# Two-layer GroupNorm and 3x3 convolution on one core: how images travel between HBM and SBUF, and when the scaled weights are written

## The chip, the cores and the metric

One core of one Trainium2 chip. The metric is device time in microseconds (us) of one execution. The times shown are the median of three runs, and one more execution was taken with the profiler.

## The reference

64 images of 256 x 256 pixels with 16 channels, fp32, 4.19 MB an image. Two layers of the same kind follow each other:

```python
x = x + relu(conv3x3(gn(x), u0, v0, w0) + b0)   # gn: 8 groups, mean and variance over the whole image
x = x + relu(conv3x3(gn(x), u1, v1, w1) + b1)   # kernel ijkl = sum u[l,j] * w[l,k] * v[l,i]
```

Each layer needs the statistics of its whole input image before it can start. The kernel never normalises the pixels: it multiplies the weights by the inverse deviation and subtracts the mean's contribution as a bias.

## The kernel before

An image is held as 128 partitions, each with two image rows (`raw[128, a, 4096]`, where a, the row parity, is 0 or 1). DVE transposes 32x32 blocks of it into `N0` ("evens"), which layer 0 convolves; the sum of layer 0 goes to `T1` ("odds"), which layer 1 convolves; that layer's sum goes to `T2` ("result") and DVE transposes it back to `pixels`, whence it is stored.

Each layer of an image is cut into four **rounds** f = 0 to 3 (`conv0(p, f)`, `conv1(p, f)`), a round being 8 pairs of image columns in each of four quarters of the width. A round is: 96 products into `ps_y` on PE (L343 for layer 1, L301 for layer 0), the bias and ReLU on ACT from `ps_y` (L426, L423), 32 products on PE that bring the unconvolved pixels into `ps_x` (L368, L323), and on DVE the sum of both (`add`, L528 and L531). PE may write `ps_y` again once ACT has read it, and `ps_x` once DVE has read it. In the program each of these products is two matmul instructions with two weight loads, so PE executes about 512 instructions a round.

The order of one pass of the loop over p is written out by hand and is the same on all engines: four rounds of layer 0 on image p, during which DVE also turns image p + 1 in (`turn_in`, L515), and then four rounds of layer 1 on image p - 1, during which DVE turns the result out (`turn_out`, L543, two transposes a round, one for each parity).

In the rounds of layer 1 the statistics of the next images are worked in. At the middle of the 96 products (`HOOK_AFTER`) of round 1 PE does `group_sums(1, p)` and in round 2 `group_sums(0, p + 1)` (L256), and each waits there until DVE has reduced the partial sums (`reduce_partials`, L558 to L564), which it does behind `turn_out` of the round before. In rounds 1 and 2 DVE scales the weights (`scale_weights`, L580 to L588), also behind `turn_out`. With the scaled weights of layer 0 ACT writes the padding of the next image (`pad_evens`, L434) between its ReLU of round 2 and that of round 3.

The transfers are all issued by SP. `load(p)` waits until image p - 1 is wholly turned in and then issues 11 DMAs, ten of 12 partitions and one of 8, each partition's two rows (32 KB) in one contiguous piece. `store(p - 1)` waits until that image is wholly turned out and issues 11 of the same kind. `turn_in` waits for all of a load, and `turn_out` of round 0 for all of the store before. `GROUPS`, `STRIDE` and `ENGINES` (12) describe this split.

POOL adds chunks of the turned image for the mean (`folds`, L237, seven additions an image) and copies the halos.

Of the kernel before, what the change touches and what calls it, by code (L numbers as in the profile page):

```python
# [7 lines left out]
IMAGES, H, W, C = 64, 256, 256, 16  # L8
P = 128
Q = 32  # L10
QUADS = 4
# [6 lines left out]
EACH = 8  # L18
ROUNDS = SLOTS // EACH
HQ = H // QUADS  # L20
HALVES = 2
# [10 lines left out]
PRM = Q * (1 + SIDES + TAPS) + 1  # L32
CST = Q * (SIDES + SIDES + 1) + 2

ENGINES = 12
STRIDE = P // ENGINES
GROUPS = [slice(o, o + (ENGINES - 1) * STRIDE + 1, STRIDE) for o in range(STRIDE)] + [slice(ENGINES * STRIDE, P)]
IN_DMAS, OUT_DMAS = len(GROUPS), len(GROUPS)
TURNS = HALVES * ROUNDS + 1
HALO0, HALO1 = 2 * (QUADS - 1), QUADS  # L40
ODDS_SUM, ODDS_PAD = 1, 2
EVENS_SUM = 2
# [3 lines left out]
def freed(f):  # L46

    return slice(max(EACH * f - 1, 0), SLOTS if f == ROUNDS - 1 else EACH * (f + 1) - 1)
# [41 lines left out]
def build(nc, x, params, consts, out):  # L90
# [2 lines left out]
    ACT = mybir.ActivationFunctionType  # L93
    AX = mybir.AxisListType

    x_rows = x.rearrange("n (g a) w c -> n g (a w c)", a=HALVES)
    out_rows = out.rearrange("n (g a) w c -> n g (a w c)", a=HALVES)

    with ExitStack() as ctx:
        def sb(name, shape):  # L100
# [9 lines left out]
        pixels = sb("pixels", [P, HALVES, ROW])  # L110
# [29 lines left out]
        const_in = sem("const_in")  # L140
        zeros_set = sem("zeros_set")
        build_step = sem("build_step")
        image_in = sem("image_in")
        image_out = sem("image_out")
        turned_in = sem("turned_in")
        halo0 = sem("halo0")
        halo1 = sem("halo1")
# [21 lines left out]
        @block.sync  # L169
        def _(sp):  # L170
            for y in range(2):
                sp.dma_start(par[y][:], params[y]).then_inc(const_in, 16)
            sp.dma_start(cst[:], consts).then_inc(const_in, 16)

            def load(p):
                if p:
                    sp.wait_ge(turned_in, TURNS * p)
                for g in GROUPS:
                    sp.dma_start(raw[g, :, :].rearrange("p a x -> p (a x)"), x_rows[p][g, :]).then_inc(image_in, 16)

            def store(p):
                sp.wait_ge(turned_out, HALVES * ROUNDS * (p + 1))
                for g in GROUPS:
                    sp.dma_start(out_rows[p][g, :],  # L184
                                 pixels[g, :, :].rearrange("p a x -> p (a x)")).then_inc(image_out, 16)

            load(0)
            load(1)
            for p in range(IMAGES):
                if p + 2 < IMAGES:  # L190
                    load(p + 2)
                if p:
                    store(p - 1)
            store(IMAGES - 1)
            sp.wait_ge(image_out, 16 * OUT_DMAS * IMAGES)

        @block.gpsimd
        def _(pool):
# [280 lines left out]
        def _(dve):  # L479
# [26 lines left out]
                    make(nc.vector.tensor_tensor(pad, whole, pad, ALU.subtract))  # L506

            def turn_in(p, f):
                dve.wait_ge(image_in, 16 * IN_DMAS * (p + 1))
                if p:  # L510
                    dve.wait_ge(x_filled, round_of(0, p - 1, f) + 1)
                turned = N0[:, :, 1:1 + HQ].rearrange("p k (g a) -> p a k g", a=HALVES)
                for a in range(HALVES):
                    pixels_in = raw[:, a, :].rearrange("p (q k x) -> p q k x", q=QUADS, x=Q)
                    nc.vector.transpose(  # L515
                        turned[:, a, 1:1 + PAIRS, :].rearrange("p (q k) g -> p q k g", q=QUADS)[:, :, freed(f), :],
                        pixels_in[:, :, freed(f), :]).then_inc(turned_in, 1)
                if f == ROUNDS - 1:
                    nc.vector.transpose(turned[:, :, 0, :], raw[:, :, ROW - Q:ROW]).then_inc(turned_in, 1)

            def add(y, p, f):
                n = round_of(y, p, f)
                dve.wait_ge(relued, n + 1)
                dve.wait_ge(x_filled, n + 1)
                if y:
                    if ROUNDS * p + f:
                        dve.wait_ge(turned_out, HALVES * (ROUNDS * p + f))
                    nc.vector.tensor_tensor(T2[:].rearrange("p q k h -> p q (k h)"), ps_x[:], R[:],  # L528
                                            ALU.add).then_inc(added, 1)
# [73 lines left out]
            for p in range(IMAGES + 1):  # L603
                if p < IMAGES:
                    for f in range(ROUNDS):
                        if f == 0:
                            take_bias(0, p)
                        add(0, p, f)
                        if p + 1 < IMAGES:
                            turn_in(p + 1, f)  # L610
                for f in range(ROUNDS):
                    if p and f == 0:
                        take_bias(1, p - 1)
                    if p < IMAGES and f == ODDS_SUM:
# [8 lines left out]
                    if p < IMAGES and f == ODDS_SUM:  # L623
                        scale_weights(1, p)
                    if p + 1 < IMAGES and f == EVENS_SUM - 1:
                        reduce_partials(0, p + 1)
                    if p + 1 < IMAGES and f == EVENS_SUM:
                        scale_weights(0, p + 1)


def constants():
# [42 lines left out]
```

## Time and profile before

| | |
|---|---|
| median of 3 runs | 5731.84 us (5716.73 to 5732.2) |
| the profiled execution, its own time | 5744.38 us |
| its span | 5742.6 us |
| PE busy, matmuls | 4926.0 us, 86% of the span |
| DVE, ACT, POOL busy | 47%, 38%, 22% |
| the last chain, by engine | PE 73%, "issue" 15%, DVE 6%, ACT 3% |
| DMA queue q1 (images) | 537.22 MB, 37.7% of 16 engines |
| DMA queue q8 (instructions) | 17.94 MB in 1095 packets, 1.3% of 16 engines |

The time outside the span is 5744.38 - 5742.6 = 1.8 us. "issue" in the chain is time in which an engine waited for nothing that the profile names. The queue q8 is the one that brings the engines their instructions. A round can be followed by the start of its ReLU on ACT, of which there are eight an image.

### The profile page before, as it was taken

The numbers are of one execution on the slowest core, as the hardware profiler recorded it, in microseconds if no ns is written. First come the engines' busy times: TensorE is split into PE (matmuls) and PEld (weight loads), VectorE is DVE, ScalarE is ACT, GpSimd is POOL, SyncE is SP. The second block draws the span as 40 slices with busy tenths as digits, with TensorE's granted clock in tenths as the row PEclk, the third lists the DMA queues.
The fourth block names the chain that finished last, engine by engine and source line by source line (L and its number), as shares of the span: only waits on it lengthen the run. The fifth ranks groups of instructions, "written<-read, shape, count | busy, mean of one in ns | idle before, by whom it ended". The sixth has DMA issues, their size and how long they took to land.

```text
span 5742.6 us, 290853 instructions
## 1 busy us (share of the span) xinstructions
PE 4926.0 (86%) x139776; PEld 2691.7 (47%) x139776; DVE 2719.5 (47%) x3148; ACT 2197.5 (38%) x2242; POOL 1260.7 (22%) x1093
## 2 busy tenths in 40 slices
PE   4888988888888889889889888898888988888886
PEld 2444444444445444445445444454444544444543
DVE  3444444445444444445444444444444544455453
ACT  2443433434334344344344343343333433434332
POOL 2222212222122222122122221221212212222120
PEclk9999999999989999999999999999999999999998
DMA  4333443334333443343443343334433433344322
GB/s 91 91 91 91 105 107 91 91 91 116 96 91 92 107 103 94 95 109 96 102 109 91 95 112 96 91 94 109 99 91 91 113 99 91 91 100 111 91 69 84
DMA packets 34378, 555.84 MB, mean 97 GB/s; under 512 B 16432, under 2 KB 16816, under 8 KB 16816
## 3 DMA queue, kind: packets, MB, share of 16 engines
q1 hardware_dynamic: 33200, 537.22, 37.7%
q8 instruction: 1095, 17.94, 1.3%
q14 instruction: 83, 0.68, 0.0%
HBM read 268.72 MB, written 268.44 MB: 94 GB/s over the span
## 4 chain that ended last, share of the span: by engine, by line
PE 73%; issue 15%; DVE 6%; ACT 3%; SPq 0%; DMA 0%; DVEq 0%; ACTq 0%
PE ps_y L343 26%; PE ps_y L301 24%; PE ps_x L368 8%; PE ps_x L323 8%; PE ps_y L305 3%; DVE pixels L543 3%; DVE result L528 3%; ACT relu L426 2%; PE ps_y L275 2%; PE ps_x L256 1%; ACT evens L434 1%; DVE scaled L588 0%; ACT relu L423 0%; SPq L184 0%; PE ps_x L266 0%
## 5 line engine op out<-in xcount | busy, mean ns | idle before, releaser
L343 PE MATMUL ps_y<-odds,scaled 32*32 32x512 f32 x49152 | 2025.2, 660 | 222.8 <-issue 217.7
L301 PE MATMUL ps_y<-evens,scaled 32*32 32x512 f32 x46080 | 1801.1, 601 | 92.3 <-issue 79.9
L343 PEld LDWEIGHTS ps_y<-odds,scaled 32*32 32x32 f32 x49152 | 899.3, 108 | 1117.9 <-issue 739.3
L528 DVE TENSOR_TENSOR result<-ps_x,relu 128x2048 f32<-128x2048 f32 x256 | 586.6, 2291 | 1472.6 <-PE ps_x L368 1016.7
L426 ACT ACTIVATE relu<-ps_y,bias 128x2048 f32<-128x2048 f32 x256 | 503.7, 1967 | 1802.3 <-PE ps_y L343 1634.9
L531 DVE TENSOR_TENSOR odds<-ps_x,relu 128x2048 f32<-128x2048 f32 x256 | 586.7, 2292 | 1278.3 <-PE ps_x L323 952.9
L301 PEld LDWEIGHTS ps_y<-evens,scaled 32*32 32x32 f32 x46080 | 825.9, 103 | 699.6 <-issue 297.1
L237 POOL TENSOR_TENSOR fold<-fold,evens 128x1024 f32<-128x1024 f32 x384 | 843.9, 2198 | 644.0 <-DVE evens L515 607.0
L368 PE MATMUL ps_x<-odds,constants 32*32 32x512 f32 x16384 | 840.2, 642 | 88.3 <-issue 80.6
L423 ACT ACTIVATE relu<-ps_y,bias 128x2048 f32<-128x2048 f32 x256 | 503.6, 1967 | 1027.2 <-PE ps_y L301 542.0
L323 PE MATMUL ps_x<-evens,constants 32*32 32x512 f32 x16384 | 775.1, 604 | 21.7 <-issue 21.3
L224 POOL COPY odds<-odds 32x256 f32<-32x256 f32 x256 | 101.4, 396 | 2969.9 <-DVE odds L531 2958.0
L515 DVE STREAM_TRANSPOSE evens<-raw 128x1024 f32<-128x1024 f32 (+2 forms) x512 | 627.9, 1270 | 25.1 <-DMA raw<-in_x 25.1
L543 DVE STREAM_TRANSPOSE pixels<-result 128x1024 f32<-128x1024 f32 x512 | 610.8, 1234 | 27.1 <-DMA out<-pixels 18.4
L399 ACT ACTIVATE junk<-odds 128x2048 f32<-128x2048 f32 x256 | 490.5, 1916 | 327.0 <-DVE odds L531 327.0
L368 PEld LDWEIGHTS ps_x<-odds,constants 32*32 32x32 f32 x16384 | 415.2, 106 | 305.9 <-issue 170.2
L399 ACT ACTIVATE junk<-evens 128x2048 f32<-128x2048 f32 (+2 forms) x256 | 487.7, 1905 | 0.8 <-DVE evens L515 0.5
L323 PEld LDWEIGHTS ps_x<-evens,constants 32*32 32x32 f32 x16384 | 365.0, 103 | 204.7 <-issue 88.3
L305 PE MATMUL ps_y<-evens,scaled 32*32 32x448 f32 x3072 | 405.9, 549 | 29.7 <-ACT relu L426 21.6
L256 PE MATMUL ps_x<-sums,constants 32*32 32x2 f32 x4096 | 61.1, 182 | 331.6 <-issue 270.1
L237 POOL TENSOR_TENSOR fold<-evens 128x1024 f32<-128x1024 f32 x64 | 152.9, 2389 | 698.5 <-DVE evens L515 698.5
L256 PEld LDWEIGHTS ps_x<-sums,constants 32*32 32x32 f32 x4096 | 50.0, 113 | 438.4 <-issue 428.0
(46 smaller groups left out, 1523.0 us busy)
## 6 DMA issues: line engine op xcount, KB each, us to landing
raw<-in_x SPq DMA_DIRECT2D x640, 384.0 KB
out<-pixels SPq DMA_DIRECT2D x640, 384.0 KB
raw<-in_x SPq DMA_DIRECT2D x64, 256.0 KB
out<-pixels SPq DMA_DIRECT2D x64, 256.0 KB
parameters<-in_params SPq DMA_DIRECT2D x2, 96.5 KB, 2.1
constants<-in_consts SPq DMA_DIRECT2D x1, 81.0 KB, 2.2
```

The source lines that it names most:

```text
L237: nc.gpsimd.tensor_tensor(to, chunk(0) if d == 1 else to, chunk(d), ALU.add).then_inc(folded, 1)
L301: done = nc.tensor.matmul(ps_y[part, r, :], w0[rows, t * Q:(t + 1) * Q], N0[rows, k:k + EACH, i:i + HQ], start=(t == 0), stop=(t == NTAP - 1))
L305: nc.tensor.matmul(ps_y[part, r, HQ:WIDE], w0[rows, t * Q:(t + 1) * Q], N0[rows, k + 1:k + EACH, i:i + HQ], start=(t == 0), stop=False, sk ...
L323: done = nc.tensor.matmul(ps_x[Q * q:Q * (q + 1), r, :], perm[Q * r:Q * (r + 1), side, :], N0[Q * r:Q * (r + 1), k:k + EACH, 1:1 + HQ], st ...
L343: done = nc.tensor.matmul(ps_y[Q * r:Q * (r + 1), q, :], w1[p % 2][Q * q:Q * (q + 1), t * Q:(t + 1) * Q], t1[Q * q:Q * (q + 1), k:k + EACH ...
L368: done = nc.tensor.matmul(ps_x[Q * r:Q * (r + 1), q, :], perm[Q * q:Q * (q + 1), side, :], t1[Q * q:Q * (q + 1), k:k + EACH, 1 + HQ * r:1 ...
L399: nc.scalar.activation(into, source, ACT.Square, accum_out=to).then_inc(squared, 1)
L426: ins = nc.scalar.activation(R[:], ps_y[:], ACT.Relu, bias=bias[:, 1:2])
L515: nc.vector.transpose(turned[:, a, 1:1 + PAIRS, :].rearrange("p (q k) g -> p q k g", q=QUADS)[:, :, freed(f), :], pixels_in[:, :, freed(f) ...
L528: nc.vector.tensor_tensor(T2[:].rearrange("p q k h -> p q (k h)"), ps_x[:], R[:], ALU.add).then_inc(added, 1)
L531: nc.vector.tensor_tensor(T1[p % 2][:, EACH * f:EACH * (f + 1), 1:1 + H].rearrange("p k (r h) -> p r k h", h=HQ), ps_x[:].rearrange("p r ( ...
L543: nc.vector.transpose(to[:, :, EACH * f:EACH * (f + 1), :], result[:, a, :, :].rearrange("p (q k) g -> p q k g", q=QUADS)).then_inc(turned ...
```

## The change

The transfers are cut by round and parity: one load or store moves, for one parity a, the column pairs of one round for all 128 partitions (128 x 4 pieces of 256 elements, 224 in the first and 288 in the last load of an image), 16 transfers an image instead of 22. SP issues one load and one store a round: the load once PE has finished the round before (`x_filled`), the store once PE has finished the round's 96 products (`y_filled`). Each transfer also waits for its own data to be ready or free, and for the last transfer of the same kind and parity. There is a semaphore for each parity. DVE waits for the piece that it is about to read or overwrite, for every transpose. On DVE, `scale_weights` moves from behind `turn_out` to ahead of it.

```diff
-            def load(p):
-                if p:
-                    sp.wait_ge(turned_in, TURNS * p)
-                for g in GROUPS:
-                    sp.dma_start(raw[g, :, :].rearrange("p a x -> p (a x)"), x_rows[p][g, :]).then_inc(image_in, 16)
+            def load(p, f, a):
+                if p >= IMAGES:
+                    return
+                if p:
+                    sp.wait_ge(turned_in, TURNS * (p - 1) + (TURNS if f == ROUNDS - 1 else HALVES * (f + 1)))
+                if ROUNDS * p + f:
+                    sp.wait_ge(image_in[a], 16 * (ROUNDS * p + f))
+                part = slice(Q * freed(f).start, Q * freed(f).stop)
+                sp.dma_start(raw[:, a, :].rearrange("p (q y) -> p q y", q=QUADS)[:, :, part],
+                             x_rows[p, a][:, :, part]).then_inc(image_in[a], 16)
+            def store(p, f, a):
...
+                sp.wait_ge(turned_out, HALVES * (ROUNDS * p + f) + a + 1)
+                if ROUNDS * p + f:
+                    sp.wait_ge(image_out[a], 16 * (ROUNDS * p + f))
...
+            def pass_on(n, loaded, stored):
+                if n:
+                    sp.wait_ge(x_filled, n)
+                load(*loaded)
+                sp.wait_ge(y_filled, n + 1)
+                store(*stored)
...
+                if p < IMAGES:
+                    pass_on(round_of(0, p, 0), (p + 1, 3, 1), (p - 2, 1, 1))
+                    pass_on(round_of(0, p, 1), (p + 2, 0, 0), (p - 2, 2, 0))
...
+                    pass_on(round_of(1, p - 1, 3), (p + 2, 3, 0), (p - 1, 1, 0))
...
             def turn_in(p, f):
-                dve.wait_ge(image_in, 16 * IN_DMAS * (p + 1))
...
                 for a in range(HALVES):
+                    dve.wait_ge(image_in[a], 16 * (ROUNDS * p + f + 1))
...
             def turn_out(p, f):
-                if f == 0 and p:
-                    dve.wait_ge(image_out, 16 * OUT_DMAS * p)
                 for a in range(HALVES):
+                    if p:
+                        dve.wait_ge(image_out[a], 16 * (ROUNDS * (p - 1) + f + 1))
...
                     if p:
                         add(1, p - 1, f)
+                    if p < IMAGES and f == ODDS_SUM:
+                        scale_weights(1, p)
+                    if p + 1 < IMAGES and f == EVENS_SUM:
+                        scale_weights(0, p + 1)
+                    if p:
                         turn_out(p - 1, f)
```

What stands in SP's program for one image in the middle, before: a store and the next load, each of 11 DMAs in a row behind one wait.

```order
L184 DMA out<-pixels 12x8192 [waits turned_out]
L184 DMA out<-pixels 12x8192 x9
L184 DMA out<-pixels 8x8192
L179 DMA raw<-in_x 12x8192 [waits turned_in]
L179 DMA raw<-in_x 12x8192 x9
L179 DMA raw<-in_x 8x8192
```

And with the change, about four of the sixteen transfers of each pass:

```order
L179 DMA raw<-in_x 128x4x256 [waits image_in0,turned_in,x_filled]
L189 DMA out<-pixels 128x4x256 [waits image_out0,turned_out,y_filled]
L179 DMA raw<-in_x 128x4x256 [waits image_in1,turned_in,x_filled]
L189 DMA out<-pixels 128x4x256 [waits image_out1,turned_out,y_filled]
L179 DMA raw<-in_x 128x4x288 [waits image_in0,turned_in,x_filled]
```

Loads and stores now alternate, each behind a signal of PE. On DVE, rounds 2 and 3 of layer 1 before (the sum, the two transposes, then the four steps that scale layer 0's weights):

```order
L528 TENSOR_TENSOR result<-ps_x,relu 128x2048 [waits turned_out,x_filled,relued]
L543 STREAM_TRANSPOSE pixels<-result 128x4x256 [waits added]
L543 STREAM_TRANSPOSE pixels<-result 128x4x256
L580 TENSOR_SCALAR small<-small 128x1 [waits rooted]
L582 TENSOR_SCALAR small<-small 128x1 [waits norm_step]
L583 TENSOR_TENSOR scale<-small 128x1 [waits norm_step]
L588 TENSOR_SCALAR scaled<-weights,scale 128x448 [waits norm_step]
L528 TENSOR_TENSOR result<-ps_x,relu 128x2048 [waits turned_out,x_filled,relued]
```

The same place with the change (its line numbers are 36 higher):

```order
L564 TENSOR_TENSOR result<-ps_x,relu 128x2048 [waits turned_out,x_filled,relued]
L616 TENSOR_SCALAR small<-small 128x1 [waits rooted]
L618 TENSOR_SCALAR small<-small 128x1 [waits norm_step]
L619 TENSOR_TENSOR scale<-small 128x1 [waits norm_step]
L624 TENSOR_SCALAR scaled<-weights,scale 128x448 [waits norm_step]
L579 STREAM_TRANSPOSE pixels<-result 128x4x256 [waits image_out0,added]
L579 STREAM_TRANSPOSE pixels<-result 128x4x256 [waits image_out1]
L564 TENSOR_TENSOR result<-ps_x,relu 128x2048 [waits turned_out,x_filled,relued]
```

The four scaling steps have moved ahead of the two transposes, and each transpose has a wait of its own for a store.

## Rows read from the trace of the kernel before

**Rows 1.** The page: span, one DMA issue with KB each and us to landing.

```profile
span 5742.6 us, 290853 instructions
...
parameters<-in_params SPq DMA_DIRECT2D x2, 96.5 KB, 2.1
```

**Rows 2.** Stretches, load then store: PE, PEld, DVE, ACT, POOL busy; clock, DMA share, GB/s.

```profile
2296.00:2320.00 24.00, 15.80 (x430) 7.09 (x414) 11.20 (x18) 5.95 (x5) 7.19 (x9) 0.86 0.74 161
...
2343.00:2361.00 18.00, 15.35 (x455) 7.18 (x425) 8.99 (x6) 9.81 (x10) 2.00 (x5) 1.00 0.71 212
```

**Rows 3.** DMA queues, 2296 to 2320 us (a load): packets, MB, share.

```profile
q8 instruction: 3, 0.05, 1.0%
```

**Rows 4.** DMA queues, 2325 to 2341 us (no image moves).

```profile
q8 instruction: 4, 0.07, 1.7%
```

**Rows 5.** The chain, 2280 to 2400 us: start, us, what.

```profile
2301.26 1.99 issue
...
2304.77 3.09 issue
...
2357.08 1.85 issue
```

**Rows 6.** ACT in order of time, image from 5118.73 us: ReLU starts, padding.

```profile
5118.73 1.97 ACT L426 ACTIVATE relu<-ps_y,bias 128x2048 f32<-128x2048 f32 x1 [2.37 <-issue]
...
5145.60 1.97 ACT L426 ACTIVATE relu<-ps_y,bias 128x2048 f32<-128x2048 f32 x1 [13.45 <-PE ps_y L343]
...
5153.61 1.09 ACT L434 ACTIVATE evens<-zeros,moments 32x129 f32<-32x129 f32 x2 [4.61 <-DVE scaled L588]
5154.72 1.97 ACT L426 ACTIVATE relu<-ps_y,bias 128x2048 f32<-128x2048 f32 x1
...
5199.03 1.97 ACT L426 ACTIVATE relu<-ps_y,bias 128x2048 f32<-128x2048 f32 x1 [2.37 <-issue]
```

**Rows 7.** ACT: ReLU of layer 1, round 0, of the first and last image but one.

```profile
169.95 1.97 ACT L426 ACTIVATE relu<-ps_y,bias 128x2048 f32<-128x2048 f32 x1 [2.36 <-issue]
...
5634.51 1.97 ACT L426 ACTIVATE relu<-ps_y,bias 128x2048 f32<-128x2048 f32 x1 [2.37 <-issue]
```

**Rows 8.** The chain, 5118 to 5200 us.

```profile
5126.74 3.32 PE ps_y L343 x91
...
5135.55 3.73 issue
5139.28 0.37 PE ps_x L256 x22
5139.66 5.88 PE ps_y L343 x96
```

**Rows 9.** DVE in order of time, same image.

```profile
5139.04 0.15 DVE L559 TENSOR_REDUCE sums<-partial 128x1 f32<-128x4 f32 x1
...
5153.12 0.46 DVE L588 TENSOR_SCALAR scaled<-weights,scale 128x448 f32<-128x448 f32 x1
```

**Rows 10.** Busy time by stretch: round 1 to 2 of that image.

```profile
5130.10:5145.60 15.50, 11.77 (x306) 5.71 (x299) 7.44 (x14) 2.06 (x2) 0.00 (x0) 0.78 0.67 142
```

**Rows 11.** Busy time by stretch: round 0 to 1 of another image.

```profile
3874.40:3887.10 12.70, 10.72 (x305) 5.78 (x294) 5.77 (x10) 4.09 (x4) 7.37 (x9) 0.87 0.74 163
```

**Rows 12.** DVE in order of time, start and end of the program.

```profile
32.96 9.13 DVE L515 STREAM_TRANSPOSE evens<-raw 128x896 f32<-128x896 f32 x8 [25.08 <-DMA raw<-in_x]
...
53.72 1.22 DVE L558 TENSOR_REDUCE sums<-fold 128x1 f32<-128x1024 f32 x1 [11.50 <-POOL fold L237]
...
5694.58 2.37 DVE L543 STREAM_TRANSPOSE pixels<-result 128x1024 f32<-128x1024 f32 x2 [18.38 <-DMA out<-pixels]
```

**Rows 13.** ACT, last image: ReLU of layer 1, rounds 0 and 3.

```profile
5671.74 1.97 ACT L426 ACTIVATE relu<-ps_y,bias 128x2048 f32<-128x2048 f32 x1 [6.83 <-PE ps_y L343]
...
5711.02 1.97 ACT L426 ACTIVATE relu<-ps_y,bias 128x2048 f32<-128x2048 f32 x1 [9.23 <-PE ps_y L343]
```

**Rows 14.** SP's issues at the end of the program.

```profile
5717.96 17.76 SPq L184 DMA_DIRECT2D out<-pixels  x11
```

More of the change, by code:

```diff
@@ L33 @@
 CST = Q * (SIDES + SIDES + 1) + 2
[L35 to L38, printed above, removed]
 TURNS = HALVES * ROUNDS + 1
@@ L94, in build @@
     AX = mybir.AxisListType
-    x_rows = x.rearrange("n (g a) w c -> n g (a w c)", a=HALVES)
-    out_rows = out.rearrange("n (g a) w c -> n g (a w c)", a=HALVES)
+    x_rows = x.rearrange("n (g a) (q w) c -> n a g q (w c)", a=HALVES, q=QUADS)
+    out_rows = out.rearrange("n (g a) (q w) c -> n a g q (w c)", a=HALVES, q=QUADS)
     with ExitStack() as ctx:
@@ L142, in build @@
         build_step = sem("build_step")
-        image_in = sem("image_in")
-        image_out = sem("image_out")
+        image_in = [sem(f"image_in{a}") for a in range(HALVES)]
+        image_out = [sem(f"image_out{a}") for a in range(HALVES)]
         turned_in = sem("turned_in")
@@ L173, in _ @@
             sp.dma_start(cst[:], consts).then_inc(const_in, 16)
-            def load(p):
+            def load(p, f, a):
+                if p >= IMAGES:
+                    return
                 if p:
-                    sp.wait_ge(turned_in, TURNS * p)
-                for g in GROUPS:
-                    sp.dma_start(raw[g, :, :].rearrange("p a x -> p (a x)"), x_rows[p][g, :]).then_inc(image_in, 16)
[L181 to L191, printed above, removed]
-                if p:
-                    store(p - 1)
-            store(IMAGES - 1)
-            sp.wait_ge(image_out, 16 * OUT_DMAS * IMAGES)
+                    sp.wait_ge(turned_in, TURNS * (p - 1) + (TURNS if f == ROUNDS - 1 else HALVES * (f + 1)))
+                if ROUNDS * p + f:
+                    sp.wait_ge(image_in[a], 16 * (ROUNDS * p + f))
@@ new lines, in load @@
+                part = slice(Q * freed(f).start, Q * freed(f).stop)
+                sp.dma_start(raw[:, a, :].rearrange("p (q y) -> p q y", q=QUADS)[:, :, part],
+                             x_rows[p, a][:, :, part]).then_inc(image_in[a], 16)
+            def store(p, f, a):
+                if p < 0:
+                    return
+                sp.wait_ge(turned_out, HALVES * (ROUNDS * p + f) + a + 1)
+                if ROUNDS * p + f:
+                    sp.wait_ge(image_out[a], 16 * (ROUNDS * p + f))
+                part = slice(Q * EACH * f, Q * EACH * (f + 1))
+                sp.dma_start(out_rows[p, a][:, :, part],
+                             pixels[:, a, :].rearrange("p (q y) -> p q y", q=QUADS)[:, :, part]
+                             ).then_inc(image_out[a], 16)
@@ new lines, in pass_on @@
+            def pass_on(n, loaded, stored):
[4 more added lines that the diff above has]
+                store(*stored)
+            for p in range(2):
+                for f in range(ROUNDS):
+                    for a in range(HALVES):
+                        if p == 0 or f < ROUNDS - 1 or a == 0:
+                            load(p, f, a)
+            for p in range(IMAGES + 1):
+                if p < IMAGES:
+                    pass_on(round_of(0, p, 0), (p + 1, 3, 1), (p - 2, 1, 1))
+                    pass_on(round_of(0, p, 1), (p + 2, 0, 0), (p - 2, 2, 0))
+                    pass_on(round_of(0, p, 2), (p + 2, 0, 1), (p - 2, 2, 1))
+                    pass_on(round_of(0, p, 3), (p + 2, 1, 0), (p - 2, 3, 0))
+                else:
+                    store(p - 2, 1, 1)
+                    store(p - 2, 2, 0)
+                    store(p - 2, 2, 1)
+                    store(p - 2, 3, 0)
+                if p:
+                    pass_on(round_of(1, p - 1, 0), (p + 2, 1, 1), (p - 2, 3, 1))
+                    pass_on(round_of(1, p - 1, 1), (p + 2, 2, 0), (p - 1, 0, 0))
+                    pass_on(round_of(1, p - 1, 2), (p + 2, 2, 1), (p - 1, 0, 1))
+                    pass_on(round_of(1, p - 1, 3), (p + 2, 3, 0), (p - 1, 1, 0))
+                else:
+                    load(p + 2, 1, 1)
+                    load(p + 2, 2, 0)
+                    load(p + 2, 2, 1)
+                    load(p + 2, 3, 0)
@@ L197, in _ @@
+            store(IMAGES - 1, 1, 1)
+            for f in (2, 3):
+                for a in range(HALVES):
+                    store(IMAGES - 1, f, a)
+            for a in range(HALVES):
+                sp.wait_ge(image_out[a], 16 * ROUNDS * IMAGES)
         @block.gpsimd
@@ L622, in _ @@
                         reduce_partials(1, p)
-                    if p < IMAGES and f == ODDS_SUM:
-                        scale_weights(1, p)
                     if p + 1 < IMAGES and f == EVENS_SUM - 1:
                         reduce_partials(0, p + 1)
-                    if p + 1 < IMAGES and f == EVENS_SUM:
-                        scale_weights(0, p + 1)
 def constants():
```

## The prediction

> **What bounds the kernel now.** I read the page first: PE is busy for 86% of the span and fills 73% of the last chain, so the rounds of PE set the time, and what matters is what stands between its products. Then ACT in order of time. The ReLU of layer 1's round 0 starts at 169.95 us in the first pass that has both layers and at 5634.51 in the last; 62 images lie between [rows 7], so an image takes (5634.51 - 169.95) / 62 = 88.14 us on average. But one image in that run took only 5199.03 - 5118.73 = 80.30 us [rows 6]. Nothing in the program differs between the two. The question is where the 7.84 us go.
>
> The chain of the end shows two kinds of "issue". One stands directly ahead of the group sums (2301.26, 1.99 us [rows 5]; 5135.55, 3.73 us [rows 8]): PE waits there for DVE. DVE ends its reduction at 5139.04 + 0.15 = 5139.19, and the group sums start at 5139.28 [rows 8, 9]. The other stands in the middle of a round's products, where the program waits for nothing: 3.09 us at 2304.77 and 1.85 us at 2357.08 [rows 5]. The first of these lies in a load, the second in a store [rows 2]. I looked at the queues there. In 24 us of the load q8 delivered 3 packets of instructions, in 16 us without image traffic it delivered 4 [rows 3, 4]: one in 8.0 us against one in 4.0. The program has 290853 instructions in 1095 such packets, 266 in each, and PE wants some 512 a round, so about 1.9 packets a round, one every 4.6 us. So PE runs out of instructions while the images' 32 KB pieces fill the DMA engines. A round that begins with such a hole, or a hole beside it, also shows a lower clock: 0.86 in that load, 1.00 in the store [rows 2].
>
> **Edit 1, transfers by chunk and parity.** It removes 22 DMAs an image and adds 16. Bytes are unchanged: 2 x 4.19 = 8.39 MB an image. No piece is longer than 1.15 KB where it was 32 KB, and no more than one load and one store of 0.52 MB are issued a round. At the rates of before, 161 GB/s and 212 GB/s [rows 2], a load takes 3.3 us and a store 2.5 us, so 5.8 us of a round of about 8.9 has image traffic, as against 4.19 MB / 161 + 4.19 MB / 212 = 46 of 88 us today. The total of the traffic is the same; what changes is how long an instruction packet stands behind it. Today it comes 4 us late (8.0 - 4.0). If what it waits for is a fixed number of pieces, the wait falls with the piece by 32; if it is everything queued, it waits for one load at most, 3.3 us, or for both, 5.8. The first end costs nothing. At the other end the delay would be about that of today, but once in a transfer and not for a whole 24 us load, with a quiet stretch behind it in which the queue catches up. I take no loss, because the store, whose pieces leave faster, already starves PE less (15.35 of 18 us busy against 15.80 of 24 [rows 2]). So the stalls go: 7.84 us an image.
>
> The Trainium skill (Runtime: NRT & Kernel Launch, Instruction fetch mechanics) says that instructions come in 16 KiB blocks over the sequencer's own DMA queue and that the cost of a block is mostly hidden. The size agrees with this trace (0.07 MB in 4 packets [rows 4]), "mostly hidden" does not, by the 3.09 us. By that sentence the holes would have another cause and edit 1 would save only the ends of the program, as in the second rival below.
>
> What stays is worth as much care. In rounds 0 to 2 of layer 1 PE waits for DVE's partial sums even in the clean image: round 1 to 2 took 15.50 us [rows 10], of which 3.73 are that wait [rows 8]. DVE does the sum, `turn_out`, `scale_weights` and `reduce_partials` in a row; the change swaps the middle two, so the reduction ends at the same time and this wait stays. The 96 matmuls behind it took 5.88 us at the lower clock; the same piece of a round, after the shorter wait in round 0 to 1, took 3.32 [rows 8], and the stretch's mean clock was 0.78 [rows 10]. In another image round 0 to 1 fell too: 12.70 us at 0.87 [rows 11], where the clean image needed 26.87 - 15.50 = 11.37 [rows 6, 10]. These are PE's own idle times, not the DMA's, so I leave them in: the clean image is the forecast for every image. Its bounds are 80.30 - (5.88 - 3.32) = 77.74 if the clock holds, and 80.30 + 12.70 - 11.37 = 81.63 if it falls twice.
>
> New waits. Each load is issued seven rounds before `turn_in` needs it (three for the last piece of an image), each store at least three before `turn_out` needs its place: over 25 us for a transfer of about 3. SP's queue holds a store behind a load's waits; the longest of these is for `turn_in` in the round just begun, which DVE does within about 5 us, ahead of `y_filled`. Each second transpose now carries a wait that is long met; I count it as nothing to 0.1 us, twice an image on PE's path, at most 12 us in all.
>
> **Edit 2, weights scaled ahead of the transposes.** In round 2 DVE ends the scaling at 5153.12 + 0.46 = 5153.58 [rows 9], ACT pads from 5153.61 for 1.09 us, and the ReLU of round 3 starts at 5154.72, directly behind it [rows 6]. So padding holds up the ReLU. That round took 5154.72 - 5145.60 = 9.12 us, where the five behind it took (5199.03 - 5154.72) / 5 = 8.86 [rows 6], one of them with extra products. Two transposes earlier the padding falls where ACT is idle (4.61 us before it [rows 6]). Gain: 0.26 to, at most, the 1.09 of the padding; I take 0.35. The transposes move back by about 1.1 us, into the 5154.72 + 1.97 - 5153.58 = 3.1 us in which DVE now waits for the end of that ReLU [rows 6, 9]. In round 1 nothing waits for it.
>
> **The ends of the program.** At the start DVE waits for the whole first image until 32.96, and reduces at 53.72, 20.8 us later, held by POOL's additions [rows 12]. With chunks the additions can start after four of eight transfers, 2.1 MB, which at 161 GB/s is half of the time: about 13 us less, and the transposes run under the load, 5 to 9 us less. I take 20. At the end, `turn_out` of the last image waits 18.38 us for the store before [rows 12]; its last three rounds took 5711.02 - 5671.74 = 39.28 us [rows 13] where 3 x 8.86 = 26.6 would do: 12.7 less. The last store is issued from 5717.96 [rows 14] and the span ends 24.6 us later; two transfers of 0.52 MB need 5.0 us at 212 GB/s and 2.1 to land [rows 1], 7.0 in all: 17.6 less.
>
> **Sum**, against the profiled execution's own 5744.4 us: an image goes from 88.14 to 80.30 - 0.35 = 79.95, times 62 is 508; 508 + 20 + 12.7 + 17.6 = 558; 5744.4 - 558 = 5186 us. The profiled execution was 12.6 us above the median of the three runs (5731.84). I don't take this off: stalls that come and go are what the change should remove.
>
> **The rivals.**
> *Half of the stalls stay* (chance 0.14). Every instruction packet now meets traffic, where today half of them do. For: a round has 5.8 us of traffic, and two packets. Against: the store's shorter occupancy. Time: 5186 + 62 x 3.92 = 5429.
> *The holes are not the images' doing, or follow the bytes* (0.07). Then 7.84 us an image stays and only the ends and the padding are won: 5186 + 486 = 5672.
> *The clock holds* (0.07). With fewer holes PE arrives busier at the wait for the group sums: 5186 - 62 x 2.56 = 5027. Against: in the clean image it fell although nothing had starved PE just before.
> *Small pieces make the transfers the bound* (0.05), the slower side. The price of 1 KB pieces is in no row at this size. The nearest is 96.5 KB in pieces of 0.8 KB, landed in 2.1 us [rows 1], which is 46 GB/s if all of it grows with the bytes (11.4 us a transfer, two a round), and nearly free if it is a fixed delay. The other end is today's 161 to 212 GB/s. I take the latter, since that row moves a fifth of the bytes. The rival decides from 8.39 MB / 88.9 us = 94 GB/s, 5.6 us a transfer with none overlapped; at 90 GB/s an image takes 93.2 us: 5186 + 62 x 13.3 = 6008. The Trainium skill (DMA: Bandwidth & Descriptors, Rules for kernel authors) asks for 1 MiB or more in a DMA, which speaks against halves of that; by its fit of 2.0 us + bytes / 436 GB/s a transfer would be, as an estimate from that page, 3.2 us and sixteen 51 us, still under an image's 80.
>
> **How the numbers follow.** The forecast has 0.67, with a range of its own from 5100 to 5280 (the clock's 81.63 adds 104 at most if in every image, a clock that holds in half of the images takes 80). The range of eight in ten, 5080 to 5440, takes in the half-stalled case and leaves out the clock that always holds, the stalls that all stay and the slower case, 0.19 together. A difference under 0.3% (17 us) can't be told from none. Faster has 0.93, all but the slower case and a bit of the second rival; same 0.02; slower 0.05.
>
> **What would show it.** Right: ReLU starts of layer 1's round 0 about 80 us apart and evenly so; q8 with two packets a round throughout; no "issue" in the middle of a round's products; the wait ahead of the group sums still about 2 and 4 us; padding done before the ReLU of round 3 is due; group sums of the first image at about 34 us; 7 us from the last transpose to the end. Wrong: holes of a microsecond in the rounds that have a load, PE or DVE waiting for a DMA in the middle of the program, or SP issuing for more than a few us a transfer.

## The result: 5173 us against 5724

The changed kernel takes 5173.18 us (median of 4 runs, 5165.69 to 5176.38), the one before 5724.28 us beside it. The ratio is 0.9036, 95% interval 0.9015 to 0.9057. The profiled execution took 5165.69 us, with a span of 5163.9. (PE does the matrix products, DVE and POOL work element by element, ACT applies the ReLU, and SP issues the transfers.)

Lines of the page of the changed kernel: its engines, its last chain and two of its DMA issues (KB each, median us to landing):

```profile
span 5163.9 us, 291702 instructions
...
PE 4731.3 (92%) x139776; PEld 2677.6 (52%) x139776; DVE 2715.9 (53%) x3148; ACT 2198.9 (43%) x2242; POOL 1261.3 (24%) x1093
...
PE 88%; issue 9%; ACT 0%; DVE 0%; ACTq 0%; DVEq 0%
...
out<-pixels SPq DMA_DIRECT2D x512, 512.0 KB, 3.5
raw<-in_x SPq DMA_DIRECT2D x256, 512.0 KB, 3.9
```

"issue" went from 15% to 9% of the chain, and DVE (6%) and ACT (3%) have fallen under 1%. A transfer of 512 KB lands 3.5 to 3.9 us after its issue.

ACT in order of time: the ReLU of layer 1's round 0 in the first and the last of the 62 images, as in [rows 7]:

```profile
134.48 1.97 ACT L462 ACTIVATE relu<-ps_y,bias 128x2048 f32<-128x2048 f32 x1 [2.37 <-issue]
...
5088.39 1.97 ACT L462 ACTIVATE relu<-ps_y,bias 128x2048 f32<-128x2048 f32 x1 [2.37 <-issue]
```

An image takes (5088.39 - 134.48) / 62 = 79.90 us, 8.24 less, which is 511 of the 579 us between the two spans. The start gives 169.95 - 134.48 = 35.5, and what follows the last of these ReLUs 108.1 - 75.5 = 32.6. The images have also become even: each takes 78.3 to 82.3 us, where before they took 80.3 to 94.7.

The chain of one image of the changed kernel, from the sum of round 2 on:

```profile
2329.22 0.48 PE ps_y L341 x4
...
2334.55 0.51 issue
...
2339.86 5.99 PE ps_y L337 x168
...
2378.12 2.00 issue
2380.12 0.33 PE ps_x L292 x19
2380.45 4.71 PE ps_y L379 x88
...
2387.47 3.34 PE ps_y L379 x92
2390.81 3.60 issue
2394.41 0.33 PE ps_x L292 x18
2394.74 4.70 PE ps_y L379 x89
```

Read beside [rows 5, 8]: of the holes of up to 3 us in the middle of products one of half a microsecond is left in this image, in round 0 of layer 0 (2334.55). The two waits ahead of the group sums (L292) are what they were, 2.00 and 3.60 us, and the products behind them are slow in both rounds of this image (4.7 us; at the full clock 3.3). The stretches of the second wait and of the products behind it (us, then busy time of PE, PEld, DVE, ACT and POOL, granted clock, DMA share, GB/s):

```profile
2390.80:2394.40 3.60, 0.01 (x1) 0.03 (x1) 3.50 (x5) 0.00 (x0) 0.00 (x0) 1.00 0.00 0
2394.70:2399.60 4.90, 4.90 (x120) 3.11 (x125) 0.70 (x4) 0.00 (x0) 0.00 (x0) 0.65 0.01 3
```

PE is idle, DVE is not, no image moves, and after it the clock falls from 2.4 GHz to 1.2 for a part of the products (mean 0.65). Over the 62 images this fall follows the second wait in every one, and the first wait in 18 of them. Before, it came in 46 images in the round of the first wait and in 60 in that of the second (rounds with over 1 us at 1.2 GHz). The time at 1.2 GHz went from 9.9 us an image to 5.1.

The next table holds the mean time between two ReLUs, worked out from the ReLU starts on ACT of 62 images in each trace. Column "1-2" is from the ReLU of layer 1's round 1 to that of round 2, "3-0'" from layer 1's last to layer 0's first.

```
kernel                0-1    1-2    2-3    3-0'   0'-1'  1'-2'  2'-3'  3'-0   image
before              14.66  17.11   9.37   9.33   9.69   9.96   9.14   8.89   88.14
changed             11.68  14.47   8.75   9.77   8.79   8.76   8.76   8.92   79.90
scale only          14.68  17.07   8.91   9.34   9.65   9.94   9.03   8.89   87.50
transfers only      11.96  14.60   9.11  10.11   8.76   8.74   8.76   8.91   80.94
unpaced             12.17  15.57   9.15   9.44   8.77   9.49  10.12   8.98   83.67
burst, small        13.22  15.59   9.10   9.33  10.93   9.77   8.73   8.89   85.56
paced, long         13.60  15.23   9.20   9.81   9.71   9.02   9.23   9.35   85.15
pairs               12.15  14.33   8.95  10.52   8.93   8.79   8.94   9.05   81.67
quiet round         11.60  14.44   8.74   9.38   8.96   8.74   8.78   8.93   79.57
reduce first         9.45  10.63   8.80   9.83   8.74   8.76   8.80   8.98   73.98
reduce + quiet       9.50   9.84   8.87   9.48   9.00   8.78   8.79   8.97   73.24
later sums           9.17   9.31   9.19   9.42   9.04   8.77   8.79   8.97   72.67
```

### The profile page after: what moved, and what is told of

It is laid out like the page before. It is cut to its first block, busy times and chain, and to the rows that moved or that the text cites. A ratio compares the mean times of both kernels' runs of the same rounds, so it can differ in the third digit from the quotient of the medians.

```text
span 5163.9 us, 291702 instructions
## 1 busy us (share of the span) xinstructions
PE 4731.3 (92%) x139776; PEld 2677.6 (52%) x139776; DVE 2715.9 (53%) x3148; ACT 2198.9 (43%) x2242; POOL 1261.3 (24%) x1093
## 3 DMA queue, kind: packets, MB, share of 16 engines
q8 instruction: 1095, 17.94, 1.5%
## 4 chain that ended last, share of the span: by engine, by line
PE 88%; issue 9%; ACT 0%; DVE 0%; ACTq 0%; DVEq 0%
PE ps_y L379 35%; PE ps_y L337 26%; PE ps_x L404 11%; PE ps_x L359 9%; PE ps_y L341 4%; PE ps_y L311 2%; PE ps_x L292 1%; PE ps_x L302 0%; ACT relu L459 0%; PE ps_y L317 0%; ACT relu L462 0%; DVE result L564 0%; DVE pixels L579 0%; ACTq L457 0%; DVEq L95 0%
## 5 line engine op out<-in xcount | busy, mean ns | idle before, releaser
L379 PE MATMUL ps_y<-odds,scaled 32*32 32x512 f32 x49152 | 1876.0, 645 | 3.8 <-issue 0.5
L337 PE MATMUL ps_y<-evens,scaled 32*32 32x512 f32 x46080 | 1741.9, 598 | 11.6 <-issue 2.4
L379 PEld LDWEIGHTS ps_y<-odds,scaled 32*32 32x32 f32 x49152 | 879.0, 106 | 820.2 <-issue 414.8
L404 PE MATMUL ps_x<-odds,constants 32*32 32x512 f32 x16384 | 776.7, 606 | 0.0
L404 PEld LDWEIGHTS ps_x<-odds,constants 32*32 32x32 f32 x16384 | 425.8, 103 | 158.2 <-issue 23.2
L359 PEld LDWEIGHTS ps_x<-evens,constants 32*32 32x32 f32 x16384 | 383.8, 103 | 155.1 <-issue 28.0
L292 PE MATMUL ps_x<-sums,constants 32*32 32x2 f32 x4096 | 47.1, 182 | 391.7 <-issue 355.5
L292 PEld LDWEIGHTS ps_x<-sums,constants 32*32 32x32 f32 x4096 | 39.0, 112 | 503.2 <-issue 496.5
## 6 DMA issues: line engine op xcount, KB each, us to landing
parameters<-in_params SPq DMA_DIRECT2D x2, 96.5 KB, 2.0
```

Source lines behind the costliest of these rows:

```text
L337: done = nc.tensor.matmul(ps_y[part, r, :], w0[rows, t * Q:(t + 1) * Q], N0[rows, k:k + EACH, i:i + HQ], start=(t == 0), stop=(t == NTAP - 1))
L359: done = nc.tensor.matmul(ps_x[Q * q:Q * (q + 1), r, :], perm[Q * r:Q * (r + 1), side, :], N0[Q * r:Q * (r + 1), k:k + EACH, 1:1 + HQ], st ...
L379: done = nc.tensor.matmul(ps_y[Q * r:Q * (r + 1), q, :], w1[p % 2][Q * q:Q * (q + 1), t * Q:(t + 1) * Q], t1[Q * q:Q * (q + 1), k:k + EACH ...
L404: done = nc.tensor.matmul(ps_x[Q * r:Q * (r + 1), q, :], perm[Q * q:Q * (q + 1), side, :], t1[Q * q:Q * (q + 1), k:k + EACH, 1 + HQ * r:1 ...
```

## The experiments

The other table that the experiments rest on counts the DMA records and PE's pauses in the same 62 images. A stretch of traffic is one in which, averaged over 1 us, more than 4 of the 16 engines move image data. A q8 packet is counted by the start of its record, and in the next two columns by its end. Pauses are those of PE over 0.3 us, without the waits directly ahead of the group sums.

```
kernel          piece   traffic us   typical     one q8 packet per us   the same, by end     pauses us
                KB      an image     stretch us  in traffic   outside   in traffic  outside  an image
before          32      48.5         23.1        5.97         4.41      6.20        4.27     6.7
paced, long     32      53.6          5.0        5.58         4.20      6.08        3.82     3.3
burst, small     1      25.7         12.9        5.89         4.69      6.46        4.56     3.7
unpaced          1      29.2          6.4        6.35         4.35      9.30        3.90     2.3
pairs            1      29.2          3.6        4.68         4.82      8.35        3.85     0.7
changed          1      33.1          2.1        4.61         4.71      5.06        4.43     0.1
```

(The typical stretch is the median; that of "paced, long" is mixed, one stretch in ten lasts 11.4 us or more.) In the long stretches both ways of counting give about 6 us. In those of a few us the count depends on where a packet of 1.1 us is put, so there the pauses are the safer measure.

That the pauses are PE's wait for instructions can be read from the trace. Of the 169 pauses over 0.5 us in the kernel before, 166 end between 1.2 and 1.8 us after the record of a q8 packet ends; in the unpaced kernel it is 104 of 104. A moment taken at random lies in such a place in 12% of cases.

**One part alone: `e1_scale_only`.** The kernel before, with edit 2.

```diff
                     if p:
                         add(1, p - 1, f)
-                        turn_out(p - 1, f)
...
+                    if p + 1 < IMAGES and f == EVENS_SUM:
+                        scale_weights(0, p + 1)
+                    if p:
+                        turn_out(p - 1, f)
```

> The kernel before with edit 2 alone (weights scaled ahead of the transposes). Theory: the padding no longer stands ahead of the ReLU of round 3, 0.42 us an image as in the changed kernel (9.10 to 8.68), 26 us in all, ratio about 0.9955. Rival: the won time is given back in the next round, which has the densest instructions and then runs out of them (9.23 to about 9.6 or more): ratio 0.998 to 1.002.

Measured: 5701.61 us (10 runs), before 5738.87, ratio 0.9937 (0.9915 to 0.9959). Round 2-3 fell by 0.46 us, round 3-0' did not move. So the gain is not given back, and edit 2 is worth about 36 us here (24 to 49 by the interval).

**The other part alone: `e2_transfers_only`.** The changed kernel with the old order on DVE.

> The changed kernel with edit 2 undone. Theory: the round from ReLU 2 to ReLU 3 of layer 1 goes back to about 9.1, an image to 80.3, the whole to about 5199 us, ratio to before 0.908; the round after it stays at about 9.8. Rival (won time is given back): that next round goes down to about 9.4 and the whole stays at about 5175 us, ratio 0.904.

Measured: 5230.51 us, ratio 0.9118 (0.9095 to 0.9141). Against the changed kernel's 0.9036 that is 0.8% of the kernel before, 47 us, give or take 18. Round 2-3 lost 0.36 us as expected. 3-0' lost 0.34 and 0-1 0.28, which neither theory had. The loss in 0-1 is the clock's: it fell after the first wait in 33 of the 62 images, where in the changed kernel it was 18, and such a round takes 12.7 us instead of 11.1 to 11.3. ACT before the padding, in the changed kernel:

```profile
2320.27 1.19 ACT L482 ACTIVATE odds<-odds,edge,constants 32x256 f32<-32x256 f32 x2
...
2323.66 1.09 ACT L470 ACTIVATE evens<-zeros,moments 32x129 f32<-32x129 f32 x2 [2.20 <-DVE scaled L624]
...
2327.11 1.97 ACT L462 ACTIVATE relu<-ps_y,bias 128x2048 f32<-128x2048 f32 x1 [2.36 <-PE ps_y L379]
```

The padding ends at 2324.75 and the ReLU now waits for PE, 2.36 us, where it stood directly behind the padding in [rows 6].

**No pacing: `e3_unpaced`.** The changed kernel, with SP not waiting for PE.

```diff
             def pass_on(n, loaded, stored):
-                if n:
-                    sp.wait_ge(x_filled, n)
                 load(*loaded)
-                sp.wait_ge(y_filled, n + 1)
                 store(*stored)
```

> The changed kernel without PE's signals on SP: a transfer goes as soon as its data are there and the last of its kind and parity has landed. Theory (short pieces are what cures, the pacing adds little): 5170 to 5215 us, q8 never late. Rival (pacing keeps the instruction packets on time): several us of holes an image come back, 5300 us or more.

Measured: 5388.21 us, ratio 0.939 (0.9362 to 0.9419). The theory that short pieces suffice has fallen: 215 us come back. SP's queue in order of time shows what the signals did:

```profile
2027.27 0.37 SPq L179 DMA_DIRECT2D raw<-in_x  x1
2027.72 0.46 SPq L189 DMA_DIRECT2D out<-pixels  x1
2028.28 0.46 SPq L179 DMA_DIRECT2D raw<-in_x  x1
2028.83 1.53 SPq L189 DMA_DIRECT2D out<-pixels  x1
```

Four transfers, 2.1 MB, are issued within about 3 us, and the next group 9 us later. The chain behind them:

```profile
2031.57 2.28 PE ps_y L334 x57
2033.85 0.52 issue
...
2041.43 2.28 PE ps_y L334 x57
2043.71 1.17 issue
```

The holes come 6.6 and 7.5 us after the first transfer of a group (2027.27 and 2036.26), in the middle of layer 0's products.

**Short pieces in the old bursts: `e4_burst_small`.** The kernel before, each whole-image load and store cut by round and parity as in the change (in equal cuts of 256) but issued at once. The store is cut in the same way.

```diff
-                for g in GROUPS:
-                    sp.dma_start(raw[g, :, :].rearrange("p a x -> p (a x)"), x_rows[p][g, :]).then_inc(image_in, 16)
+                for f in range(ROUNDS):
+                    for a in range(HALVES):
+                        part = slice(Q * EACH * f, Q * EACH * (f + 1))
+                        sp.dma_start(raw[:, a, :].rearrange("p (q y) -> p q y", q=QUADS)[:, :, part],
+                                     x_rows[p, a][:, :, part]).then_inc(image_in, 16)
```

> The kernel before with its whole-image loads and stores kept as bursts, but each cut into 8 DMAs of 128 x 4 pieces of 1 KB. Theory (an instruction packet waits for a fixed number of pieces, so short pieces cure): an image takes about 80.5 us, start and end as before, about 5240 us, ratio 0.915. Rival (it waits for whatever bytes are queued): as before or worse, 5700 us, ratio about 1.

Measured: 5535.54 us, ratio 0.965 (0.9621 to 0.9678), between the two theories. A load and a store as stretches (columns as above):

```profile
2033.00:2047.00 14.00, 11.68 (x359) 5.59 (x347) 5.78 (x10) 4.08 (x3) 8.98 (x9) 1.00 0.94 299
2078.50:2091.00 12.50, 11.32 (x344) 5.48 (x327) 4.46 (x5) 4.06 (x4) 1.59 (x4) 1.00 0.96 313
```

The queues in the first of them (packets, MB, share of 16 engines):

```profile
q1 hardware_dynamic: 4185, 4.16, 92.7%
q8 instruction: 2, 0.03, 0.9%
```

The rate is 299 and 313 GB/s, where [rows 2] had 161 and 212 with 32 KB pieces in groups of 12 partitions. But in 14 us PE still got 2 packets of instructions, 7 us each. The piece is 32 times shorter, and the packet comes no sooner: one in 5.89 us in traffic against 5.97. What the new cut bought is that the traffic is over in half the time, 25.7 us an image instead of 48.5: the DMA share is 0.94 and 0.96 where it was 0.74 and 0.71 [rows 2].

**Long pieces, paced: `e5_paced_long`.** The kernel before, its 11 DMAs issued one or two at each signal of PE, the stores over layer 0's rounds and the loads over layer 1's (shown).

```diff
+                            sp.wait_ge(x_filled, n)
+                            some(p + 2, FIRST[f], True)    # two of the 11 DMAs
+                            sp.wait_ge(y_filled, n + 1)
+                            some(p + 2, SECOND[f], True)   # one
```

> The kernel before with its 32 KB pieces and its 11 DMAs an image, but issued one or two at a time by PE's signals: stores over the four rounds of layer 0, loads over the four of layer 1. Theory (the length of the piece decides): an instruction packet still waits for pieces of 2.4 us, now in all rounds; holes stay at over half, 5450 to 5700 us. Rival (what decides is how much is queued): holes gone, about 80.5 us an image, about 5240 us.

Measured: 5551.38 us, ratio 0.966 (0.963 to 0.969). Holes are spread over all rounds. It stands within the range of the theory of long pieces. The count allows another reason, and beside `e4_burst_small` it is the likelier: these transfers are so slow that even paced they fill 53.6 us of an image, half of their stretches last 5 us or more, and the packets come one in 5.58 us.

**Dose: `e8_pairs`.** The changed kernel, the same 16 transfers, signalled two loads and two stores at a time in every second round.

```diff
+                held.append((loaded, stored))
+                if len(held) < 2:
+                    return
+                sp.wait_ge(x_filled, n)
+                for one, _ in held:
+                    load(*one)
+                sp.wait_ge(y_filled, n + 1)
+                for _, one in held:
+                    store(*one)
```

> The changed kernel, its transfers unchanged in size and count, but signalled in pairs: every second round two loads at once, then two stores at once. New theory (an instruction packet is late in proportion to how long image traffic runs without a break: stretches of 2 us harmless, of 6 us and more one packet in 6 us): stretches of about 4 us, part of the loss of the unpaced kernel, 5200 to 5320 us, ratio 0.91 to 0.93. Rival (what hurt the unpaced kernel is loads and stores at the same time, which pairs don't bring): 5165 to 5185 us, ratio 0.903.

Measured: 5271.73 us, ratio 0.9187 (0.9161 to 0.9213), as the new theory had it. An image takes 81.67 us, 1.77 more than with single signals, over a third of it in 3-0' (10.52). Only the grouping differs, so grouping alone costs 1.5% of the kernel before. The pauses rise from 0.1 to 0.7 us an image, and the clock falls after the first wait in 38 images instead of 18.

**The hole that is left: `e7_quiet_round`.** The changed kernel, nothing issued during the 96 products of layer 0's round 0.

```diff
+                if late:
+                    sp.wait_ge(y_filled, n + 1)
+                    load(*loaded)
+                    sp.wait_ge(x_filled, n + 1)
+                    store(*stored)
+                    return
```

> The changed kernel with no new transfer issued during the first half of layer 0's round 0, the round with the most instructions: its load waits for the end of the 96 products, its store for the end of the round. Theory (what is left of the holes lies there: 9.77 us on average against 9.23 at least): that round goes to about 9.4, 20 to 30 us less in all, about 5148 us. Rival (the spread of that round is not the transfers'): 5173 us. The store that the round before issues at its y_filled lies before this round's products and stays.

Measured: 5147.46 us, ratio 0.8975 (0.8957 to 0.8993), 0.6% below the change's 0.9036: 35 us by the ratios, give or take 16, and 20 between the two spans. 3-0' went from 9.77 to 9.38; 0.17 of it came back in the next round, which now has both transfers.

**The wait that stayed: `e6_reduce_first`.** The changed kernel with the reduction ahead of the transposes.

```diff
+                    if p < IMAGES and f == ODDS_SUM - 1:
+                        reduce_partials(1, p)
+                    if p + 1 < IMAGES and f == EVENS_SUM - 1:
+                        reduce_partials(0, p + 1)
                     if p:
                         turn_out(p - 1, f)
-                    if p < IMAGES and f == ODDS_SUM - 1:
-                        reduce_partials(1, p)
-                    if p + 1 < IMAGES and f == EVENS_SUM - 1:
-                        reduce_partials(0, p + 1)
```

> The changed kernel with reduce_partials moved ahead of the two transposes of turn_out in rounds 0 and 1 of layer 1. Theory (the wait ahead of the group sums is DVE's chain of sum, transposes, reduction): both waits end 2.4 us earlier, the first goes to nearly nothing (2.0) and the second from 3.6 to 1.2, with less time at the lower clock: 4.4 to 6 us an image, 4800 to 4900 us. Rival (something else releases it, such as ACT's squares or POOL's additions): under 1 us an image, over 5110 us.

Measured: 4795.45 us, ratio 0.8362 (0.8345 to 0.8379). That is just under the 4800 to 4900 expected. An image takes 73.98 us, 5.92 less than in the changed kernel. The chain:

```profile
2065.62 0.33 PE ps_x L292 x18
2065.95 2.89 PE ps_y L379 x77
...
2074.76 1.36 issue
2076.12 0.33 PE ps_x L292 x19
2076.45 2.89 PE ps_y L379 x78
```

The first wait is gone, the second is 1.36 us, and the products behind both take 2.9 us. The mean granted clock is 0.997, against 0.967 in the changed kernel: with the two waits the falls of the clock went too, in all 62 images.

**The best version: `e9_reduce_quiet` and `e10_later_sums`.** The first adds the quiet round and puts the reduction ahead of `scale_weights` as well. The second also lets PE make the group sums 16 products later (`if t == HOOK_AFTER + (f > 0)`).

> The changed kernel with reduce_partials directly behind the sum, ahead of scale_weights and the transposes, and with the quiet first half of layer 0's round 0. Theory: the second wait ahead of the group sums falls by 1.0 us more (from 1.35), and that round by 0.4: 1.3 to 1.5 us an image below reduce first alone, about 4710 us, ratio 0.822. Rival (the next thing in line, ACT's squares or POOL's additions, holds the reduction): 4770 us.

> As the last one, with PE's group sums of rounds 1 and 2 one tap (16 products) later. Theory: the rest of the wait, 0.3 to 0.5 us in round 2, is gone, at most 25 us: about 4690 us. Rival (the wait is already gone, later sums only push DVE's variance behind): 4710 us or more.

Measured: 4748.43 us, ratio 0.8276 (0.8254 to 0.8298), and 4712.37 us, ratio 0.8211 (0.8187 to 0.8235). The first fell short of its 4710 and came nearer to its rival's 4770: round 1-2 gained 0.79 us and 3-0' 0.35, but 0'-1' gave back 0.26. The second missed its 4690, which was reckoned from 4710, but gained 36 us where at most 25 were expected: 0-1 and 1-2 fell by 0.33 and 0.53, and 2-3 rose by 0.32. Its page:

```profile
PE 4608.5 (98%) x139776; PEld 2653.6 (56%) x139776; DVE 2731.6 (58%) x3148; ACT 2199.1 (47%) x2242; POOL 1262.3 (27%) x1093
```

PE is busy for 98% of the span. This is the fastest version tried, 18% under the kernel before.

## Why the prediction was right, and where its working was not

**The image, forecast 79.95 us, measured 79.90.** The step "the clean image is the forecast for every image" held as a mean, and that it came within 0.05 us is luck: errors cancel. The holes did not go wholly: 3-0' kept 0.5 us over its clean 9.24, and the four rounds of layer 0 some 0.16 together. Against that, 1-2 took 14.47 us where the clean image had 15.50 [rows 10], since the clock was low for 4.1 us of it and not for 6.8 (a mean of 0.78 over 15.50 us), and 0-1 11.68 where that image had 11.37, since the clock fell there in 18 of the 62 images. The clean image is no floor either: the fastest of the changed kernel took 78.27 us.

**What the 8.24 us consist of.** The prediction laid its 7.84 us to holes alone. The pauses in the middle of products gave 6.6 us (6.7 to 0.1). The waits ahead of the group sums took 1.4 back: they came to 4.15 us an image before and to 5.52 after. That PE, held up by a hole, came later to such a wait and found less of it left is the likely reason, but no run tests it. PE's busy time fell from 4926.0 to 4731.3 us, 3.0 an image. About 2.4 of it is the clock, which was at half its speed for 4.7 us less. The prediction had no term for that apart from the clean image.

**Why the holes went.** The prediction named two ways in which an instruction packet could wait, for a fixed number of pieces or for what is queued, and leaned to the first, so that "the wait falls with the piece by 32". That step is wrong. Its delay of 4 us a packet was also too large: it came from 3 packets and 4, and over 62 images it is 5.97 us in traffic against 4.41 outside. With pieces of 1 KB in bursts of 13 us (`e4_burst_small`) packets come one in about 6 us, as they do with 32 KB. What the pauses go with is for how long the traffic runs without a break, and for how much of the time. With pieces of 1 KB, stretches of 12.9, 6.4, 3.6 and 2.1 us leave pauses of 3.7, 2.3, 0.7 and 0.1 us an image. Short stretches are nearly harmless, since PE has instructions in hand: what q8 has brought and PE not yet executed varies over some 500 instructions, about two packets (an estimate from the counts of both in these traces). The changed kernel needs both of its properties: the cut over 128 partitions, which shortens the traffic (299 GB/s in `e4_burst_small`), and PE's signals, which break it up. Neither alone gives much: 0.965 for the first in whole-image bursts (0.939 cut by chunk, with edit 2) and 0.966 for the second; both together, without edit 2, give 0.9118. The length of the piece and its spread over the partitions were always changed together. How an engine shares its time between two queues is not shown by these runs.

**The second end of that estimate** was a wait of 3.3 us for one load, to be caught up in the quiet behind it. That is nearer to what was seen. It suggests that what is left is lost where the instructions are densest, in layer 0's round 0 with its small extra products, and `e7_quiet_round` won 0.39 us of the 0.53 there.

**The wait ahead of the group sums stays.** Right: 2.00 and 3.60 us, where before they were 1.99 [rows 5] and 3.73 [rows 8]. `e6_reduce_first` shows that DVE's transposes stood in it, and that the falls of the clock hang on these waits. They also hang on the holes: without them the fall in the round of the first wait went from 46 images to 18. The prediction had the one hole of 1.85 us in a stretch at clock 1.00 [rows 2, 5], so a hole alone need not bring a fall. The rival in which the clock holds (5027 us) failed: both waits were still there, and the clock fell behind the second one in every image.

**Edit 2, forecast 0.35 us an image (22 us).** The mechanism was right (`e1_scale_only`), the size too small: 36 us with an interval of about 24 to 49. The round was read from one clean image, 9.12 against 8.86, and that mean of five holds rounds with extra products. The round itself went to 8.68 in the median of the changed kernel, 0.44 below. In company with edit 1 it was worth 47 us by the ratios, with an uncertainty of 18, so the two values can't be told apart. Of the 0.6 us in rounds 3-0' and 0-1 that go with it, the part in 0-1 is that the clock falls in fewer images. Why it does, and the 0.34 us in 3-0', stay open.

**The start, forecast 20 us, measured 35.5.** DVE at the start of the changed kernel:

```profile
7.81 4.57 DVE L551 STREAM_TRANSPOSE evens<-raw 128x896 f32<-128x896 f32 x4
...
19.97 1.38 DVE L551 STREAM_TRANSPOSE evens<-raw 128x1152 f32<-128x1152 f32 x1 [0.75 <-DMA raw<-in_x]
...
28.80 1.22 DVE L594 TENSOR_REDUCE sums<-fold 128x1 f32<-128x1024 f32 x1 [7.33 <-POOL fold L273]
```

The reduction comes at 28.80 instead of 53.72 [rows 12], 24.9 us earlier. The term was worked out with 161 GB/s, but the load ran faster: DVE did its first four transposes without a wait from 7.81 on, and the last of the eight transfers had landed by 19.97, where before DVE waited for the image until 32.96 [rows 12]. Another 10.6 us came between the reduction and the first image of the count. By the first ReLU 31.0 us were won (43.99 for 75.01), by the ReLU at 134.48 the 35.5. The mechanism was right and the size of the term too small.

**The end, forecast 30.3 us, measured 32.6.** The last three rounds took 5151.67 - 5125.63 = 26.04 us (forecast 26.6), and the span ends 5.3 us after the last transpose (forecast 7.0). ACT in the last image:

```profile
5125.63 1.97 ACT L462 ACTIVATE relu<-ps_y,bias 128x2048 f32<-128x2048 f32 x1 [6.83 <-PE ps_y L379]
...
5151.67 1.97 ACT L462 ACTIVATE relu<-ps_y,bias 128x2048 f32<-128x2048 f32 x1 [6.71 <-PE ps_y L379]
```

**The slower rival** asked whether small pieces could make the transfers the bound, at under 94 GB/s. In bursts they move at 299 GB/s (`e4_burst_small`), and paced they land in 3.5 to 3.9 us. The row on which the rival stood was 96.5 KB landed in 2.1 us. Five times the bytes took 1.4 to 1.8 us more, so most of the 2.1 us, about 1.7 as an estimate from these rows, was a fixed delay.

**Slips in its sums.** None moves the forecast. The clock's 81.63 was compared with 79.95, which has edit 2 in it; like with like it adds 1.33 x 62 = 82 us and not 104. The 266 instructions a packet count those of all engines; PE alone has 2 x 139776 in 1095 packets, 255 each.

## What to carry to other kernels

Look for one undisturbed pass in the trace of the kernel before: it shows what a change can reach, with the waits that stay in it, but it is one image and no floor. If PE runs through long unrolled code, count the instruction packets on their queue in traffic and out of it, and see whether its pauses end right behind one. Move data in transfers that are over within 2 to 3 us, tied to PE's progress, and keep them away from the densest code. And a short wait of PE costs more than itself: the reduction moved ahead of two transposes took 2.0 and 2.2 us off the two waits in the chains shown, but 5.9 us off an image.

## What the hardware did that was not expected

- Instruction packets were as late behind 1 KB pieces as behind 32 KB pieces: one in 5.9 us against 6.0 in traffic, and 4.2 to 4.7 outside it.
- Of 169 pauses of PE over half a microsecond 166 ended 1.2 to 1.8 us after an instruction packet had come.
- 128 x 4 pieces of 1 KB moved at 299 (load) and 313 GB/s (store), 12 partitions with 32 KB pieces at 161 and 212. The spread over the engines and the piece were changed together; no run parts them.
- After 3.6 us without products in one round the granted clock averaged 0.65 over the next 4.9 us. With the first wait gone and the second cut to 1.36 us it was 0.997 over the whole run.
